# A matrix-sort-and-layernorm pipeline on one core: the last pair's 128 rows written by one indirect transfer from GpSimd, the first key block loaded through ScalarE's queue

## The reference

```python
q, k, v = x @ Wq, x @ Wk, x @ Wv
attn = softmax(einsum('btd,bTd->btT', q, k) * V ** -0.5)
attn_out = einsum('btT,bTd->btd', attn, v) @ Wp + bp
cms_out = gelu(attn_out @ cW1 + cb1) @ cW2 + cb2 + one_hot(target_codes, V)[:, None, :]
concat = concatenate([attn_out, cms_out], axis=-1)
modifier = gelu(concat @ mW1 + mb1) @ mW2 + mb2
z = clip(x + cms_out + modifier, 0.0, 1.0)
```

```python
h = gelu(z @ W_down[role] + b_down[role])
y = z + h @ W_up[role] + b_up[role]
out = (y - mean(y)) * rsqrt(var(y) + 1e-5) * gamma[role] + beta[role]
```

## Time and profile before

| | us |
|---|---|
| median of 3 runs | 2033.6 |
| lowest, highest | 2032.85, 2033.67 |
| the profiled execution, its own time | 2032.4 |
| its span, first to last instruction | 2030.8 |

### The profile page before, as it was taken

The page is one execution under the profiler, slowest core; times in us unless marked ns, Lnnn a source line. Parts: engine busy times, 40 slices in busy tenths (PEclk is TensorE's granted clock), DMA queues, the critical chain, the costliest instruction groups (busy, mean ns, idle before and its releaser), DMA issues.

```text
span 2030.8 us, 28039 instructions
## 1 busy us (share of the span) xinstructions
PE 2005.9 (99%) x9371; PEld 1670.6 (82%) x9371; DVE 1391.9 (69%) x2601; ACT 950.2 (47%) x1977; POOL 107.4 (5%) x199
## 2 busy tenths in 40 slices
PE   8999999999999999999999999999999999999997
PEld 7888878888888888888888888888888888888896
DVE  6786786555777686556686786565686686654897
ACT  4754453433654454333564453343374454433564
POOL 0000000000000000000000000000000000000132
PEclk9999999999999999999999999999999999999999
DMA  4121233315111143125111232224311132222754
GB/s 167 32 63 42 75 123 109 94 52 202 63 52 63 52 145 109 50 90 206 65 53 48 68 116 97 89 94 152 118 35 60 53 114 99 94 74 75 247 162 116
DMA packets 113024, 193.79 MB, mean 95 GB/s; under 512 B 12393, under 2 KB 72050, under 8 KB 108404
## 3 DMA queue, kind: packets, MB, share of 16 engines
q1 hardware_dynamic: 98404, 128.42, 20.1%
q0 software_dynamic: 14400, 63.46, 8.9%
q10 hardware_dynamic: 80, 0.13, 0.0%
HBM read 148.71 MB, written 43.26 MB: 95 GB/s over the span
## 4 chain that ended last, share of the span: by engine, by line
PE 91%; DVE 5%; DMA 2%; issue 1%; SPq 1%; ACT 0%; DVEq 0%; POOL 0%; POOLq 0%
PE y L1712 16%; PE y L1714 15%; PE y L1713 15%; PE x L1712 13%; PE x L1714 13%; PE x L1713 13%; PE y L1801 1%; PE x L1826 1%; DVE w_lo L1145 1%; DMA bet<-beta 1%; DVE c_forms L1307 1%; DMA w_blocks<-w1m 1%; PE x L2062 1%; DVE f L1211 0%; PE y L1800 0%
## 5 line engine op out<-in xcount | busy, mean ns | idle before, releaser
L693 ACT CAST w_hi<-w_blocks 128x512 fp32r<-128x512 f32 (+1 forms) x464 | 231.4, 519 | 124.6 <-PE y L1714 83.7
L1145 DVE TENSOR_TENSOR w_lo<-w_blocks,w_hi 128x512 fp32r<-128x512 f32 (+1 forms) x464 | 249.9, 564 | 54.7 <-ACT w_hi L693 54.7
L1712 PE MATMUL x<-h_hi,w_hi 128*128 128x512 f32 x512 | 199.7, 390 | 0.0
L1712 PE MATMUL y<-h_hi,w_hi 128*128 128x512 f32 x512 | 199.4, 389 | 0.0
L1713 PE MATMUL x<-h_lo,w_hi 128*128 128x512 f32 x512 | 199.3, 389 | 0.0
L1713 PE MATMUL y<-h_lo,w_hi 128*128 128x512 f32 x512 | 199.2, 389 | 0.0
L1714 PE MATMUL y<-h_hi,w_lo 128*128 128x512 f32 x512 | 199.2, 389 | 0.0
L1714 PE MATMUL x<-h_hi,w_lo 128*128 128x512 f32 x512 | 199.2, 389 | 0.0
L1712 PE MATMUL y<-a_forms,w_hi 128*128 128x512 f32 x480 | 187.9, 391 | 2.1 <-DVE f L1248 2.0
L1714 PE MATMUL y<-a_forms,w_lo 128*128 128x512 f32 x480 | 186.9, 389 | 0.0
L1713 PE MATMUL y<-a_forms,w_hi 128*128 128x512 f32 x480 | 186.8, 389 | 0.0
(11 more groups left out here) (240 smaller groups left out, 4243.2 us busy)
## 6 DMA issues: line engine op xcount, KB each, us to landing
w_blocks<-w1m SPq DMA_DIRECT2D x128, 256.0 KB, 4.5
w_blocks<-w1c SPq DMA_DIRECT2D x64, 256.0 KB, 3.2
w_st<-w2c SPq DMA_DIRECT2D x64, 256.0 KB, 3.1
w_st<-w2m SPq DMA_DIRECT2D x64, 256.0 KB, 4.7
x_hi_lo<-x_halves POOLq DMA_DIRECT2D x6, 2048.0 KB, 11.0
zs<-z_by_batch SPq DMA_DIRECT2D x66, 128.0 KB, 2.1
cms<-f SPq DMA_DIRECT2D x32, 256.0 KB, 2.8
z_cms<-cms POOLq DMA_DIRECT2D x8, 1024.0 KB, 7.0
```

Source lines behind the costliest of these rows:

```text
L693: nc.scalar.copy(w1_hi[:, w % RING, cols], src).then_inc(w1_hi_s, 1)
L1145: nc.vector.tensor_tensor(w1_lo[:, w % RING, cols], src, f32(w1_hi[:, w % RING, cols]), ALU.subtract).then_inc(w1_lo_s, 1)
L1712: nc.tensor.matmul(ps, w[0], x[0], start=first, stop=False, skip_group_check=more)
```

## The change

Two edits.

**The first key block.** Block 0 of Wk no longer goes through SyncE's list but is the first instruction of ScalarE's, ahead of the load of its function table. SyncE's further loads stand one place earlier.

The first fence is ScalarE's list (with waits) from its start, before and after; SyncE's follows.

The diff:

```diff
--- before.py
+++ after.py
@@ -113,6 +113,7 @@
     wa_dram = nc.dram_tensor("wa_blocks", (2 * DC, P, D), F32).ap()
     z_dram = nc.dram_tensor("z_by_batch", (B, P, DC * S), F32).ap()
     cf_dram = nc.dram_tensor("cms", (NT, P, DC, TOK), F32).ap()
+    last_dram = nc.dram_tensor("last_batches_row", (2, 1), I32).ap()
     wu_dram = nc.dram_tensor("wu_halves", (2, P, R * (KD // P) * D), F32).ap()
     bd_dram = nc.dram_tensor("bd_halves", (2, R * KD), F32).ap()
     x_dram = nc.dram_tensor("x_halves", (NT, 2, P, DC, TOK), F32).ap()
@@ -145,6 +146,11 @@
         ones2f = sb("ones2f", [P, P])
         ones2 = sb("ones2", [P, P], F32R)
         warm = sb("gelu_table", [P, 1])
+
+        last_b = sb("last_batches", [P, 1], I32)
+        last_f = sb("last_batches_f32", [P, 1])
+        row_s = sb("row_in_batch", [P, 1])
+        last_rows = sb("last_rows", [P, 1], I32)
         mx = sb("mx", [P, 1])
         nmx = sb("nmx", [P, 1])
         rs = sb("rs", [P, 1])
@@ -337,7 +343,7 @@
         d_mm, hgelu_s, ht_mm, ht_hi_s, ht_lo_s = sem("down_mm"), sem("down_gelu"), sem("ht_mm"), sem("ht_hi_ready"), sem("ht_lo_ready")
         u_mm, st_s, mv_s, ve_s = sem("up_mm"), sem("stats"), sem("mean_var"), sem("var_eps")
         rstd_s, yg_s, yo_s = sem("rstd"), sem("times_gamma"), sem("row_ready")
-        last_a = sem("last_first_stored")
+        last_out, last_in, rows_s, last_pair = sem("last_batches_out"), sem("last_batches_in"), sem("last_rows_ready"), sem("last_pair_stored")
         a_stored = [sem(f"first_stored{k}") for k in range(UNROLL)]
         b_stored = [sem(f"second_stored{k}") for k in range(UNROLL)]
 
@@ -373,7 +379,8 @@
 
             for k in range(DC):
                 sp.dma_start(f2[:, k, :], wqT[:, k, :]).then_inc(qk_loaded[k], 16)
-                sp.dma_start(f1[:, k, :], wkT[:, k, :]).then_inc(qk_loaded[k], 16)
+                if k:
+                    sp.dma_start(f1[:, k, :], wkT[:, k, :]).then_inc(qk_loaded[k], 16)
             sp.dma_start(h1_tile[:], wvT).then_inc(wv_loaded, 16)
             sp.dma_start(h2_tile[:], wp).then_inc(wp_loaded, 16)
             sp.dma_start(x_st[:], xT[0]).then_inc(x0_loaded, 16)
@@ -472,13 +479,12 @@
 
                 b = batch_of(second_t, n)
                 dst = out[bass.ds(b, 1)].rearrange("o s d -> (o s) d")
-                if n == NPAIR - 1:
-                    sp.wait_ge(last_a, 16)
-                else:
-                    sp.wait_ge(a_stored[u % UNROLL], 16 * (n // UNROLL + 1))
+                sp.wait_ge(a_stored[u % UNROLL], 16 * (n // UNROLL + 1))
                 sp.dma_start(dst, yo[S:2 * S, u % UNROLL, :]).then_inc(b_stored[u % UNROLL], 16)
 
             sp.wait_ge(sorted_s, 3)
+            for k in range(2):
+                sp.dma_start(last_dram[k:k + 1], (first_t, second_t)[k][0:1, NPAIR - 1:NPAIR]).then_inc(last_out, 16)
             sp.wait_ge(z1_stored, (NS - 1) * 16)
             sp.wait_ge(z2_stored, (NS - 1) * 16)
             sp.wait_ge(prod[P3], (2 * NQ - 1) * NS)
@@ -491,6 +497,9 @@
                 load_z(n, n)
             for h, half in enumerate((wu_hi, wu_lo)):
                 sp.dma_start(f32(half[:]).rearrange("p r k n -> p (r k n)"), wu_dram[h]).then_inc(wu_in, 16)
+            sp.wait_ge(last_out, 32)
+            for k in range(2):
+                sp.dma_start(last_b[k * S:(k + 1) * S, :], last_dram[k:k + 1].to_broadcast([S, 1])).then_inc(last_in, 16)
             sp.dma_start(gam[:], gamma.to_broadcast([P, R, D])).then_inc(gb_loaded, 16)
             sp.dma_start(bet[:], beta.to_broadcast([P, R, D])).then_inc(gb_loaded, 16)
 
@@ -515,9 +524,8 @@
                 if m == 4 + 2 * DC:
                     sp.wait_ge(z2_ready, DC * NS)
                     store_z(NT - 1, h1_tile, last_stored[1])
-            store_second(NPAIR - 1, NPAIR - 1)
             for u in range(UNROLL):
-                sp.wait_ge(b_stored[u], 16 * ((NPAIR - 1 - u) // UNROLL + 1))
+                sp.wait_ge(b_stored[u], 16 * ((NPAIR - 2 - u) // UNROLL + 1))
 
 
         @block.gpsimd
@@ -628,8 +636,14 @@
             for n in range(NPAIR - 1):
                 store_first(n, n)
                 inverse_std(n + 1, (n + 1) % 2)
+
+            pool.wait_ge(rows_s, 4)
+            pool.wait_ge(yo_s, NPAIR)
+            pool.indirect_dma_start(out.rearrange("b s d -> (b s) d"), bass.IndirectOffsetOnAxis(ap=last_rows[:], axis=0),
+                                    yo[:, (NPAIR - 1) % UNROLL, :], None).then_inc(last_pair, 16)
             for u in range(UNROLL):
                 pool.wait_ge(a_stored[u], 16 * ((NPAIR - 2 - u) // UNROLL + 1))
+            pool.wait_ge(last_pair, 16)
 
 
 
@@ -670,6 +684,7 @@
         @block.scalar
         def _(act):
 
+            act.dma_start(f1[:, 0, :], wkT[:, 0, :]).then_inc(qk_loaded[0], 16)
             for k in range(DC):
                 act.wait_ge(qk_loaded[k], 32)
                 nc.scalar.copy(t1[:, 0, k, :], f2[:, k, :]).then_inc(qw_hi, 1)
@@ -1027,12 +1042,6 @@
                 unit(n, n, True, True)
             for n in range(2, NPAIR):
                 unit(n, n, n + 2 < NPAIR, n + 1 < NPAIR)
-
-            b = act.value_load(first_t[0:1, NPAIR - 1:NPAIR], min_val=0, max_val=B - 1)
-            act.wait_ge(yo_s, NPAIR)
-            act.dma_start(out[bass.ds(b, 1)].rearrange("o s d -> (o s) d"),
-                          yo[0:S, (NPAIR - 1) % UNROLL, :]).then_inc(last_a, 16)
-            act.wait_ge(last_a, 16)
 
 
         @block.vector
@@ -1683,6 +1692,17 @@
                     scale_shift(n - 1, u - 1, r, reuse)
 
 
+            def last_pair_rows():
+
+                nc.vector.tensor_scalar(row_s[:], iota_p[:, 0:1], float(S), -float(S), ALU.is_ge, ALU.mult).then_inc(rows_s, 1)
+                dve.wait_ge(rows_s, 1)
+                nc.vector.tensor_tensor(row_s[:], row_s[:], iota_p[:, 0:1], ALU.add).then_inc(rows_s, 1)
+                dve.wait_ge(last_in, 32)
+                nc.vector.tensor_copy(last_f[:], last_b[:]).then_inc(rows_s, 1)
+                dve.wait_ge(rows_s, 3)
+                nc.vector.scalar_tensor_tensor(out=last_rows[:], in0=last_f[:], scalar=float(S), in1=row_s[:],
+                                               op0=ALU.mult, op1=ALU.add).then_inc(rows_s, 1)
+
 
             for n in range(NPAIR):
                 unit(n, n, n + 2 < NPAIR, n > 0, n > UNROLL)
@@ -1695,6 +1715,8 @@
                     z2_sum(s, n - 4)
                 elif n < 4 + 2 * DC:
                     z2_clip(s, n - 4 - DC)
+                elif n == 4 + 2 * DC:
+                    last_pair_rows()
             last = NPAIR - 1
             r = dve.value_load(role_t[0:1, last:last + 1], min_val=0, max_val=R - 1)
             stats(last, last)
```

## The result

The changed kernel takes 2038.19 us, the median of 15 runs; the kernel before took 2033.23 beside it. (A single run of 3148.6 us among these, and one of 2512.7 us in a later kernel, at 0.60 and 0.75 of TensorE's clock, are left out of the ratios.) The ratio is 1.0025, with a 95% interval from 1.0017 to 1.0033: the change makes the kernel slower by 5.1 us (3.5 to 6.7). Forecast was 2032.7, 0.9 faster than the 2033.6 known then, with a range of 2031.1 to 2035.0. The profiled execution of after has a span of 2036.6 us and a time of 2038.19; of before, 2030.8 and 2032.4.

A forecast was written before the change was run, and what follows sets the result against it. TensorE, busy 99%, was taken to bound the kernel, so gains could come only at its start and end. Terms -0.3 + 0.1 + 0.3 - 1.0 = -0.9 us took 2033.6 to 2032.7; range 2031.1 to 2035.0.

The forecast's parts named there:

- the sentence on the closing: End of the program: 3.2 us from the last store's landing to the span's end, left alone by the change.
- the other terms: Everything but the last pair's transfer: first key block -0.3, two broadcasts ahead of gamma and beta +0.1, four VectorE instructions +0.3.
- The indirect transfer's price: Last pair's single store by GpSimd: 3.7 us to landing, at 2026.65 instead of 2027.6, so -1.0 us; bounds -1.9 and +0.4.
- the cheap rival: Last pair's store: describing 128 rows costs nothing, 2.8 us to landing, sum -1.8, time 2031.8; chance 0.20.
- The dear one: Last pair's store: describing rows on GpSimd takes 2.9 us, 5.9 to landing, sum +1.4, time 2035.0; chance 0.15.
- slower: Whole kernel above 2037.7 us, through the indirect transfer's code or its reading of rows costing over 5 us; chance 0.05.
- The row instructions: Four small VectorE instructions ahead of unit 13's `ht_lo`: 0.65 us, making TensorE wait +0.3 us once; bounds 0 and +0.4.
- The slack of 0.34: Unit 13: `up` started 0.90 us after `ht_lo` against 0.56 in unit 12, room to cover part of VectorE's added work.
- Beta: Two broadcasts issued ahead of gamma and beta: beta issued 1.0 us later, mostly covered by queued `wu` loads, +0.1; bounds 0 and +1.0.
- The start: First key block issued by ScalarE at 0.94 instead of SyncE at 1.41: `wp` lands earlier, -0.3 us; bounds 0 and -0.5.
- the queue of bytes: Loads before `wp`: engines are full, so earlier issue helps only by 0.13 MB moved in the first microsecond, 0.3 us.
- The step before it: Start: `wp`'s landing, through VectorE's copy, sets `sort_counts` at 24.43; an earlier first product alone is worth at most 0.17 us.

## Why the prediction was wrong, point by point

**The step that failed** is the sentence on the closing: "From there to the span's end are 3.2 us of closing the program, which the change leaves alone." The 3.2 us were the difference of two things that have nothing to do with each other: the landing of SyncE's last store, and the end of a DRAIN on GpSimd that had begun 5 us before that landing. I took the last transfer for the last thing, since the engine behind it is never shown as busy, and did not look at what each engine's list ended with. The rows were in the trace of before: a DRAIN of 7827 ns from 2022.7. With them, and the prediction's own 0.65 to the issue and 3.7 from there to the landing, GpSimd is free 5.1 us behind the start of the last `yo` (0.75 + 0.65 + 3.7); with 7.8 of DRAIN and 0.3 the span ends 13.2 us behind it, where before it was 9.2: +4.0 in place of -1.0, and with the other terms as they stood (+0.1 together) 2033.6 + 4.1, that is 2037.7. Measured was a span's end 8.4 us behind the landing, not 3.2.

**The indirect transfer's price** was set too high: forecast 3.7 us from issue to landing (2.5 + 0.5, and 0.7 for describing 128 rows), measured 2.8, which is the cheap rival's price. Nothing of the 0.7 shows between issue and landing; the issue came 0.88 us behind `yo` instead of 0.65. Together the rows were there 3.7 us behind `yo` for a forecast of 4.35. The cheap rival was right in this price and wrong in the time (2031.8), since the landing did not set the end. The dear one would have ended on the right side for a wrong reason. No rival had the mechanism. The chance of 0.05 for "slower" was given to a costly transfer; a list of GpSimd's that ends 3.6 us later behind the last `yo` was in plain sight in the text of the change ("GpSimd's list now ends last").

**The row instructions**: +0.3 forecast, bounds up to +0.4; measured +0.76. The 0.65 us for the instructions were 0.60. The slack of 0.34 was there too, and the missing 0.5 is the register load that had lain beside `z_lo` and `yo`. I had asked what hides the added work, but not what the work next to it had been hiding.

**Beta**: +0.1 forecast, bounds to +1.0. Two broadcasts were counted as 1.0 us of issuing; they took 1.26, and beta's issue came 1.55 us later behind that of `wu_lo` than before (2.50 for 0.95). +0.7 in the profiles of before and after, of which the other traces make about 0.3 likely and the rest scatter.

**The start**: -0.3 forecast. The block's issue at 0.94 and the table load behind it came as said; `wp` did not land earlier (16.28 for 16.14), but it had not been issued earlier either (5.46 for 5.20), so this execution does not test the reasoning on the queue of bytes. In the three other kernels with the block on ScalarE `wp` was issued at 4.81 to 4.99 and awaited until 15.41, 15.82 and 15.84; in the seven with it on SyncE it was issued at 5.19 to 5.37 and awaited until 15.57 to 16.79 (mean 16.07). A gain of some tenths would fit and is not shown. The step before it failed more plainly: that the landing of `wp`, through VectorE, is what sets `sort_counts`. It held for the trace of before, by less than 0.2 us; in eight of the eleven traces, after among them, `sort_counts` waits for no copy of VectorE's, and TensorE's own pace sets it. In after it was 1.07 us later. Over all eleven traces it came at 24.43 to 25.82 us, with the block on SyncE (24.43, 24.60, 24.61, 25.07, 25.09, 25.38, 25.82) as on ScalarE (24.90, 25.50, 25.50, 25.74): TensorE's slow beginning varies by over 1 us between executions. By the times, the start's part is worth +0.0003 of the whole (-0.0006 to +0.0012). That the edit prolongs the slow stretch by some tenths is neither shown nor excluded.

The account of the +5.1 us: +3.7 for the tail, which the table shows, +0.8 for the row instructions, which three traces show in one place, perhaps 0.3 for beta; the 0.3 that are left lie within the interval of 3.5 to 6.7.

## What to carry to other kernels

Before you shorten the last transfer, look up the last instruction of every engine's list: the program ends with the latest of them plus its closing, and on GpSimd that closing was 7.8 us in every kernel here, so GpSimd wants to be the first engine to finish. Give the last stores and the final waits to engines whose closing takes nanoseconds, and keep GpSimd's last work and last wait more than 8 us before the end. And when you insert short instructions, ask what the sequencer was doing under the long one next to them.

## What the runs showed of the hardware that was not expected

- GpSimd's closing DRAIN lasts 7.8 to 7.9 us, in eleven traces: 7.83 where GpSimd waited idle before it (7.91 where its last operation was the indirect transfer), and 7.8 to 7.9 from the end of the last operation where its row began beside it. It does not wait for transfers that are still on their way (the two kernels with GpSimd's waits on SyncE). SyncE's took 7 ns, ScalarE's 8 ns, but ScalarE's 401 ns where its list ended beside its last cast, and VectorE's 766 ns beside the last `yo`. Why GpSimd's is so long stays open.
- An indirect transfer of 128 rows of 2 KB by GpSimd took 1.08 us to issue and 2.8 us from issue to landing. That is the time of a direct store of the same 256 KB by SyncE. A direct issue by GpSimd took 0.56 for 128 KB, 0.54 for 256 KB and 0.72 for 2 MB, so nearly, but not wholly, the same "whatever it moves".
- A register load with its arithmetic takes VectorE's sequencer about 0.5 us (311 and 190 ns). It cost nothing beside long instructions and showed in full, 0.50 us, behind four short ones that wait for each other, in the three kernels that have them in a row.
- Two broadcasts of 4 bytes to 64 partitions held SyncE's queue for 1.26 us in after (1.1 to 1.6 in the others), and landed 9.5 us later behind the `wu` loads.
